# Weaving the row products of y with the first product of layer 1, half of the array at a time

## The reference

```python
def kan_linear(x, base_w, spline_w, scaler, grid):
    base = silu(x) @ base_w.T
    b = b_splines(x, grid)                       # 8 cubic splines per value
    return base + einsum('nik,oik->no', b, spline_w * scaler[..., None])

x1 = spectral_conv2d(x, w1, w2)                  # FFT, 2 x 16 x 16 modes mixed, inverse FFT
x2 = einsum('bchw,oc->bohw', x, conv_w) + conv_b
y  = (x1 + x2).transpose(0, 2, 3, 1).reshape(-1, 64)
y  = kan_linear(y, k1_base, k1_spline, k1_scaler, grid)
y  = kan_linear(y, k2_base, k2_spline, k2_scaler, grid)
return gelu(y.reshape(b, h, w, c).transpose(0, 3, 1, 2))
```

## Time and profile before

| | |
|---|---|
| median of 3 runs | 3722.03 us |
| profiled execution | 3726.12 us |
| its span | 3723.8 us |
| TensorE (PE) busy | 3647.0 us, 98% |
| VectorE (DVE) busy | 3483.2 us, 94% |
| ScalarE (ACT) busy | 3373.7 us, 91% |
| the chain that ended last | PE 89%, of it `l_ps` at L1167 83% |
| mean granted TensorE clock | 0.991 |

### The profile page before, as it was taken

The page is one execution under the profiler, slowest core; times in us unless marked ns, Lnnn a source line. Parts: engine busy times, 40 slices in busy tenths (PEclk is TensorE's granted clock), DMA queues, the critical chain, the costliest instruction groups (busy, mean ns, idle before and its releaser), DMA issues.

```text
span 3723.8 us, 98210 instructions
## 1 busy us (share of the span) xinstructions
PE 3647.0 (98%) x36804; PEld 1450.2 (39%) x36804; DVE 3483.2 (94%) x3548; ACT 3373.7 (91%) x3509; POOL 110.0 (3%) x131
## 2 busy tenths in 40 slices
PE   8987999999999999999999999999999999999998
PEld 4555433333333333333333333333333333333334
DVE  7874999999999999999999999999999999999997
ACT  4432998999999999999999999999999999999997
POOL 0000000000000000000000000000000000000000
PEclk9988999999999999999999999999999999999999
DMA  9997234433232232322322323223222232232231
GB/s 314 325 224 165 47 98 122 115 81 95 63 76 66 67 76 59 74 70 63 76 65 68 76 58 75 70 63 76 63 70 73 60 76 68 65 76 61 72 74 49
DMA packets 270071, 338.43 MB, mean 91 GB/s; under 512 B 83616, under 2 KB 199072, under 8 KB 267936
## 3 DMA queue, kind: packets, MB, share of 16 engines
q1 hardware_dynamic: 249136, 266.39, 25.5%
q0 software_dynamic: 18288, 66.59, 9.8%
q10 hardware_dynamic: 2560, 4.20, 0.4%
HBM read 248.50 MB, written 88.61 MB: 91 GB/s over the span
## 4 chain that ended last, share of the span: by engine, by line
PE 89%; issue 1%; DVE 0%; ACT 0%; DMA 0%; SPq 0%; ACTq 0%; DVEq 0%
PE l_ps L1167 83%; PE y_banks L1146 3%; PE y_banks L1153 2%; PE y_banks L1182 1%; PE y_banks L1130 0%; PE y_banks L1122 0%; PE y_banks L1167 0%; PE l_ps L1182 0%; DMA inv_h_sb<-inv_h_dram 0%; DVE cube0r L995 0%; ACT above L1043 0%; ACT size L1054 0%; ACT offset L1058 0%; ACT S L1047 0%; ACT below L1051 0%
## 5 line engine op out<-in xcount | busy, mean ns | idle before, releaser
L1058 ACT ACTIVATE offset<-size 128x1024 f32<-128x1024 f32 x1280 | 1240.8, 1045 | 8.1
L995 DVE SCALAR_TENSOR_TENSOR cube0r<-below,offset 128x1024 f32<-128x1024 f32 x256 | 313.5, 1225 | 131.1 <-ACT offset L1058 126.0
L995 DVE SCALAR_TENSOR_TENSOR cube2r<-below,offset 128x1024 f32<-128x1024 f32 x256 | 312.9, 1222 | 1.4 <-PE l_ps L1167 1.0
L1004 DVE SCALAR_TENSOR_TENSOR inner_cube<-below,square 128x1024 f32<-128x1024 f32 x256 | 313.4, 1224 | 0.0
L995 DVE SCALAR_TENSOR_TENSOR cube4l<-above,offset 128x1024 f32<-128x1024 f32 x256 | 313.3, 1224 | 0.0
L995 DVE SCALAR_TENSOR_TENSOR cube1r<-below,offset 128x1024 f32<-128x1024 f32 x256 | 312.7, 1221 | 0.6 <-PE l_ps L1167 0.6
L995 DVE SCALAR_TENSOR_TENSOR cube4r<-below,offset 128x1024 f32<-128x1024 f32 x256 | 313.2, 1223 | 0.0
L995 DVE SCALAR_TENSOR_TENSOR cube3l<-above,offset 128x1024 f32<-128x1024 f32 x256 | 313.1, 1223 | 0.0
L995 DVE SCALAR_TENSOR_TENSOR cube3r<-below,offset 128x1024 f32<-128x1024 f32 x256 | 313.0, 1223 | 0.0
L995 DVE SCALAR_TENSOR_TENSOR cube2l<-above,offset 128x1024 f32<-128x1024 f32 x256 | 312.9, 1222 | 0.0
L995 DVE SCALAR_TENSOR_TENSOR cube1l<-above,offset 128x1024 f32<-128x1024 f32 x256 | 312.8, 1222 | 0.0
(11 more groups left out here) (158 smaller groups left out, 5784.5 us busy)
## 6 DMA issues: line engine op xcount, KB each, us to landing
big<-in_x_dram SPq DMA_DIRECT2D x128, 512.0 KB, 7.4
x_ring<-in_x_dram SPq DMA_DIRECT2D x256, 256.0 KB, 4.4
out_dram<-act_out SPq DMA_DIRECT2D x128, 512.0 KB, 2.7
act_out<-in_x_dram POOLq DMA_DIRECT2D x127, 512.0 KB, 7.1
rows_t<-rows_scratch SPq DMA_DIRECT2D x512, 32.0 KB
rows_scratch<-rows SPq DMA_DIRECT2D x14, 1024.0 KB, 6.6
pair_t<-pair_scratch SPq DMA_DIRECT2D x128, 65.0 KB, 1.9
big<-in_spec_w_r_dram SPq DMA_DIRECT2D x16, 512.0 KB, 11.6
```

Source lines behind the costliest of these rows:

```text
L995: nc.vector.scalar_tensor_tensor(out=cube[q][side][:], in0=distance[layer][:], scalar=EDGE - KNOTS[q], in1=offset[layer][q][:], op0=ALU.mi ...
L1004: nc.vector.scalar_tensor_tensor(out=inner_cube[:], in0=below[layer][:], scalar=EDGE, in1=square[layer][:], op0=ALU.subtract, op1=ALU.mult ...
L1058: nc.scalar.activation(offset[layer][q][:], size[layer][:], ACT.Square, bias=-KNOTS[q]).then_inc(offset_ready[layer], 1)
```

## The change

The function `y_by_quarters` is split. Its conv part becomes `conv_by_quarters`, and keeps its place at the head of the step. Its rows part becomes `rows_with_product`, which is issued where layer 1's first product stands and contains it: the four quarters of the product of `S[0]` are no longer issued in one go, but two at a time. First come two row matmuls in the upper half of the array's rows (g = 0, 1; e = 0), then the two quarters of the product in the lower half (r = 1), then the other two row matmuls of the upper half (e = 1), then the two quarters of the product in the upper half (r = 0), and then the four row matmuls of the lower half (g = 2, 3). `y_done` is raised behind the last of these. The wait for `rows_loaded` moves from the head of y to the head of the woven part, and behind the wait for `S_ready[0]` of the tile that layer 1 works on. This holds for tiles 19 to 127; y of the earlier tiles is as before.

```diff
-            def y_by_quarters(src, par, like):
+            def conv_by_quarters(j, par, like):
+                pe.wait_ge(x_loaded, 48 * (j + 1))
+                pe.wait_ge(S_ready[0], j)
+                pe.sem_inc(seen, 1)
+                src = tile_of(x_ring, j)
...
+            def rows_with_product(j, par, dst):
+
+                pe.wait_ge(rows_loaded, 64 * (j + 1))
+                pe.sem_inc(seen, 1)
+
+                def of_rows(g, e):
+                    q = slice(g * 2 * MODES, (g + 1) * 2 * MODES)
+                    at = g * MM + e * W
+                    return nc.tensor.matmul(y_banks[:, at:at + W],
+                                            rows[q, par, 2 * e:2 * e + 2, :].rearrange("q i o -> q (i o)"),
+                                            inv_w4_sb[q, :], start=False, stop=(e == HG - 1), skip_group_check=True,
+                                            tile_position=(g * 2 * MODES, 0))
+
+                def of_silu(r):
+                    for n in range(TN // MM):
+                        quarter(dst, 0, F_SILU, S[0], n, r)
+
+                for g in range(2):
+                    of_rows(g, 0)
+                of_silu(1)
+                for g in range(2):
+                    of_rows(g, 1)
+                of_silu(0)
                 for e in range(HG):
-                    for g in range(ROW_GRP):
-                        q = slice(g * 2 * MODES, (g + 1) * 2 * MODES)
...
-                return ins
+                    for g in range(2, ROW_GRP):
+                        ins = of_rows(g, e)
+                ins.then_inc(y_done, 1)
...
+                woven = WIDE_FROM <= like + 2 <= last
+                if woven:
+                    conv_by_quarters(i + 2, like % 2, like + 2)
+                elif like + 2 <= last:
                     y(i + 2, like % 2, like)
...
-                    product(dst, layer, F_SILU, S[layer])
+                    if woven and layer == 0:
+                        rows_with_product(i + 2, like % 2, dst)
+                    else:
+                        product(dst, layer, F_SILU, S[layer])
```

More of the change, by code:

```diff
@@ L1110, in y @@
                 src = tile_of(x_ring, j)
[L1112 to L1116, removed]
+                y_by_halves(src, par).then_inc(y_done, 1)
             def y_by_halves(src, par):
@@ L1148, in y_by_quarters, with quarter @@
                                              skip_group_check=True, tile_position=(n * C, i * C))
-                for e in range(HG):
-                    for g in range(ROW_GRP):
-                        q = slice(g * 2 * MODES, (g + 1) * 2 * MODES)
[L1152 to L1156, removed]
-                return ins
+            def rows_with_product(j, par, dst):
[17 more added lines that the diff above has]
+                of_silu(0)
+                for e in range(HG):
+                    for g in range(2, ROW_GRP):
+                        ins = of_rows(g, e)
+                ins.then_inc(y_done, 1)
+            def quarter(dst, layer, f, src, n, r):
+                rows_, cols = slice(r * C, (r + 1) * C), slice(n * C, (n + 1) * C)
+                return nc.tensor.matmul(dst[cols, r * MM:(r + 1) * MM], kan_w[layer][rows_, f, :],
+                                        src[rows_, n * MM:(n + 1) * MM], start=(f == 0), stop=(f == NF - 1),
+                                        tile_position=(r * C, n * C))
             def product(dst, layer, f, src):
@@ L1165, in product @@
                     for r in range(2):
[L1166 to L1169, removed]
+                        ins = quarter(dst, layer, f, src, n, r)
                 return ins
@@ L1185, in step @@
             def step(i, like):
-                if like + 2 <= last:
+                woven = WIDE_FROM <= like + 2 <= last
+                if woven:
+                    conv_by_quarters(i + 2, like % 2, like + 2)
+                elif like + 2 <= last:
                     y(i + 2, like % 2, like)
```

## The result

The changed kernel takes 3939.01 us, the median of six runs (3937.28 to 3959.47). The kernel before took 3723.19 us in its six runs beside them. The ratio on record is 1.059, with a 95% interval of 1.0576 to 1.0605. By the medians it is 215.8 us slower, or 1.98 us for each of the 109 wide tiles. The profiled execution has a span of 3936.7 us, 212.9 us over before.

What follows compares the result with a forecast made beforehand. TensorE was taken to bound the kernel. Per wide tile, 0.86 us (second passage of `S`), 0.45 (row turns of two) and 0.67 (shape changes) sum to 1.98; times 109, 216 us, giving 3938 us, range 3912 to 3964.

Steps and rivals of the forecast that it cites:

- The leader: In the loop of wide tiles TensorE never waits and sets the pace, so its added work counts in full.
- some 7 us of slack: After the woven part, ScalarE reads y some 7 us after the later `y_done`, so that delay adds nothing.
- A change of shape waits for the whole array: At the step's head, a matmul of another shape starts only once the array is empty, so six pieces run in a row; 87%.
- A pair: Two changes of array shape in a step's head, one to 32 x 128 and one back: 0.34 us, ends 0.30 and 0.40.
- Two more pairs: In the woven part, three pairs of shape changes where one was: 0.67 us added a tile, ends 0.60 and 0.80.
- The second passage of `S`: In the woven part, the product of `S` issued as two pieces holds the array twice: 0.86 us added a tile.
- The rows part in turns of two: In the woven part, row matmuls run two at a time, not four, eight turns for four: 0.45 us added a tile.
- The ends of 208 and 230 us: Bounds of the added time over 109 wide tiles, from the ends of the shape changes alone: 1.91 and 2.11 us a tile.
- What would show it: Profile signs at a step's head: rows to `S` about 0.4 us, `S` to rows 1.0, head near 4.5, step 27.7.
- (a): Rival: in the woven part each half of the rows changes shape by itself, 0 to +12 us, 3728 us; 4%.
- (b): Rival: in the woven part one half's emptying and weight load hide behind the other's streaming; 40 us less, 3682 us; 4%.
- (c): Rival: half-empty array in each woven part brings one clock fall a tile, 191 us on top, 4129 us; 5%.

Runs made afterwards that it cites:

- h1: Changed kernel with all tiles making y in 64 x 64 quarters, tiles 19 to 127 still woven, so no change of shape: 3722.76 us, ratio 1.0009.
- f2: Changed kernel, still woven, with the rows part on 32 x 64 pieces in place of 32 x 128: 3920.15 us, ratio 1.0537.
- f1: Kernel before, not woven, with the wide rows part on sixteen 32 x 64 matmuls in place of eight 32 x 128: 3717.14 us, ratio 0.9990.
- e2: Changed kernel unwoven in tiles 19 to 127: four row matmuls, whole product of `S`, other four; one more pair than before: 3759.93 us, ratio 1.0105.
- e3: Changed kernel reordered in tiles 19 to 127: four row matmuls, lower half of `S`, four row matmuls, upper half of `S`: 3849.21 us, ratio 1.0346.
- e4: Changed kernel with row matmuls in one piece, upper half's four then lower half's, then whole `S`; one pair as before: 3722.31 us, ratio 1.0006.

## Why the prediction was right, step by step

- **The leader.** That TensorE never waits and that its added work is added whole held: VectorE's share of the loop is 90% (2348.10 of 2600.00), as forecast, and TensorE has no wait in the loop. ScalarE's read of y was given some 7 us of slack, and has it: it starts at 2037.54, 7.0 us behind the end of the woven part (2030.57).
- **A change of shape waits for the whole array.** This was read from the earlier trace rows. The result, h1 beside the changed kernel, and f2 beside f1 show it: the same weave costs 0 us in one shape, and 216 or 203 us across two. That matmuls of another shape are merely started in order, without a wait for the end of the stream, does not fit the changed kernel:

```profile
2027.98 0.60 PE L1180 MATMUL l_ps<-S,turned_w 64*64 64x512 f32 x2
```

These are the last records of the first half of `S`, in the lower half of the array. They stream 0.43 us, half of a product's 0.86. The rows part, in the upper half, starts 0.53 us behind them (2028.51): 0.10 us after the stream has ended.
- **The terms.** A pair: taken as 0.34 us, measured 0.36 (e2), inside its ends of 0.30 and 0.40. Two more pairs are 0.73 us where the sum had 0.67. The second passage of `S`: 0.86, measured 0.82 (e3 over e2). The rows part in turns of two: 0.45; what is left of the 1.98 us is 1.98 - 0.73 - 0.82 = 0.43, which no run measured alone. The first two terms were off by +0.06 and -0.04 us, and nearly cancelled. The third is a remainder, so it says nothing of its own, and it carries what e3's other way of paying for `S` may hide. Two of the sum's figures were rounded apart as well: half of the early rows part is 0.87 / 2 = 0.44, not 0.45, and 2 x 0.34 is 0.68, not 0.67; the sum is 1.98 either way. The ends of 208 and 230 us are what the terms allowed; that 3938 met 3939 to the microsecond is luck.
- **What would show it.** Forecast about 0.4 us from rows to `S`, 1.0 from `S` to rows, a head of 4.5 and a step of 27.7; measured 0.42, 1.01, 4.46 and 27.69.
- **The rivals.** (a), each half changing by itself, and (b), the gaps hidden behind the other half, both wanted `S` to start within 0.1 us of the first row matmuls. It starts 0.42 us behind. (c), the clock: 1.00 in the loop.
- **What the reckoning did not have.** The prediction let each half of `S` stand alone. In the changed kernel they do, since rows follow each. Where a half of `S` is followed by its own shape, as in e3, the other half of the array runs ahead with later products, and pays at the end of the step: 0.82 us all the same.

## What to carry to other kernels

In all that was run here, pieces of the array run apart only while they all have one shape; before the first matmul of another shape the whole array empties, and what stood in the other half stops being cover. So group matmuls by shape, count the changes in a step, and multiply by the price of a pair, which an experiment with one pair more gives (e2: 0.36 us). Interleaving cost nothing inside one shape (h1), and gained nothing with equal work in both halves. Whether it gains something with unequal work was not tried.

## What the runs showed of the hardware that was not expected

- Matmuls on free pieces overtake. In h1 the rows part's second pair (h = 1) is issued ahead of `S`. A quarter of the upper half takes a record every 0.11 us, two for h = 0 (2021.78 and 2021.88) and then those of h = 1, from 2021.99 on, while `S` starts in the lower half at 2021.88. In e4 four row matmuls that stood behind waiting ones cost nothing (0.67 us for 0.66). In e3 a lower quarter of `below` starts 0.02 us behind `S` in the upper half, ahead of an upper quarter of `below` that waits for it.
- The overtaking has an end: in e3, conv's first four records start from 2018.01 on in the free half, which is free again at 2018.44, and its other twelve only from 2018.81, with the later half. Why it stops there was not tried.
- It does not matter which side of the shape changes. From 64 x 64, 32 x 64 changes the rows alone and empties the array as 32 x 128 does, with 0.38 us from rows to `S` in f2 (2018.93 to 2019.31) and 0.42 in the changed kernel. 64 x 128 changes the columns alone: its pair of changes holds 0.36 us by the earlier trace rows, and it waits for a quarter that it does not use.
